# First slice of embedding rows normed and projected on its own, ahead of the lag network's last layer, in a one-core language-model tower

## What is computed

```python
h = W[x] + pe                                   # embedding
n = (h - mean(h)) / sqrt(var(h) + 1e-5)         # first layer norm
q, k, v = n @ Wq.T, *split(n @ Wkv.T)
q, k = elu(q) + 1, elu(k) + 1                   # = max(x, 0) + exp(min(x, 0))
D = 1 / max(einsum(q, k.sum(tokens)), 1e-6)
context = einsum('bhnd,bhne->bhde', k, v)
h = h + (einsum('bhnd,bhde->bhne', q, context) * D) @ Wproj.T + bproj
...
g = idx @ pos_w.T + pos_b                       # the lag network, used by the third block
for i in range(3):
    g = relu(g / (norm(g) / sqrt(8) + 1e-8)) @ rpe_lw[i].T + rpe_lb[i]
a = relu(g / (norm(g) / sqrt(8) + 1e-8)) @ out_w.T + out_b
```

## Time and profile before

| | |
|---|---|
| median of 3 runs | 337.44 us (334.92 to 338.07) |
| the profiled execution: its time | 338.1 us |
| its span from first to last instruction | 336.4 us |
| TensorE busy | 302.3 us, 90% of the span |
| VectorE busy | 231.2 us, 69% |
| ScalarE busy | 147.5 us, 44% |
| GpSimd busy | 118.7 us, 35% |
| chain that ended last | TensorE 52%, VectorE 10%, GpSimd 5%, ScalarE 3% |

### The profile page before, as it was taken

The page is one execution under the profiler, slowest core; times in us unless marked ns, Lnnn a source line. Parts: engine busy times, 40 slices in busy tenths (PEclk is TensorE's granted clock), DMA queues, the critical chain, the costliest instruction groups (busy, mean ns, idle before and its releaser), DMA issues.

```text
span 336.4 us, 4468 instructions
## 1 busy us (share of the span) xinstructions
PE 302.3 (90%) x1598; PEld 171.7 (51%) x1598; DVE 231.2 (69%) x420; ACT 147.5 (44%) x246; POOL 118.7 (35%) x167
## 2 busy tenths in 40 slices
PE   1649879999989999989899999999999999999884
PEld 1316654653333434667545556554555555557552
DVE  1578788799988684276854687744678577673676
ACT  2113543933766676455546444544532110022452
POOL 5764001332741245201402550431004689900114
PEclk9999999999999999998999999999999999999959
DMA  7959300483000003300000000000000000000001
GB/s 249 320 99 365 141 0 0 69 155 61 3 2 3 2 2 113 140 2 0 1 0 2 0 1 2 0 0 2 1 0 2 0 0 2 0 0 1 2 0 63
DMA packets 6270, 15.17 MB, mean 45 GB/s; under 512 B 1384, under 2 KB 3816, under 8 KB 5608
## 3 DMA queue, kind: packets, MB, share of 16 engines
q1 hardware_dynamic: 5685, 14.35, 14.3%
q0 software_dynamic: 512, 0.53, 0.7%
q10 hardware_dynamic: 51, 0.01, 0.0%
HBM read 11.95 MB, written 0.52 MB: 37 GB/s over the span
## 4 chain that ended last, share of the span: by engine, by line
PE 52%; DVE 10%; POOL 5%; ACT 3%; issue 2%; POOLq 0%; DVEq 0%; ACTq 0%
PE ps L325 50%; DVE arena L1856 1%; DVE h L1982 1%; POOL share L587 1%; ACT L1197 1%; PE ps L1098 1%; DVE xs L1784 1%; DVE rw L1727 1%; POOL share L588 1%; ACT arena L1304 1%; POOL st L551 0%; POOL rw L480 0%; DVE arena L1777 0%; DVE xc L2044 0%; PE ps L872 0%
## 5 line engine op out<-in xcount | busy, mean ns | idle before, releaser
L1727 DVE TENSOR_REDUCE rw<-ps 128x1 f32<-128x512 f32 (+2 forms) x80 | 45.8, 629 | 6.9 <-PE ps L325 6.4
L1315 ACT ACTIVATE arena<-ps 128x1024 f32<-128x1024 f32 (+3 forms) x48 | 37.6, 812 | 24.6 <-PE ps L325 24.1
L325 PE MATMUL ps<-arena 96*128 96x512 bf16 (+7 forms) x192 | 42.8, 327 | 0.6 <-DVE rw L1727 0.2
L1375 ACT ACTIVATE arena<-ps 128x512 f32<-128x512 f32 x48 | 28.7, 598 | 29.1 <-PE ps L325 24.8
L325 PE MATMUL ps<-xs,e_hi 128*128 128x512 f32 x96 | 41.1, 428 | 0.2 <-DVE arena L1856 0.2
L1856 DVE TENSOR_TENSOR arena<-ps,arena 128x512 f32<-128x512 f32 x48 | 32.6, 687 | 11.5 <-ACT arena L1375 10.0
L325 PE MATMUL ps<-xs,e_lo 128*128 128x512 f32 x96 | 38.4, 400 | 0.0
L325 PE MATMUL ps<-bfc_s 128*128 128x512 bf16 (+2 forms) x112 | 30.8, 356 | 1.7 <-issue 1.7
L325 PEld LDWEIGHTS ps<-arena 96*128 96x128 bf16 (+1 forms) x192 | 15.9, 98 | 26.5 <-DVE rw L1727 11.6
L494 POOL TENSOR_SCALAR_AFFINE_SELECT arena<-arena 128x256 f32<-128x256 f32 (+1 forms) x32 | 15.0, 472 | 33.3 <-ACT arena L1315 32.8
L325 PE MATMUL ps<-w,xT 128*128 128x128 f32 (+2 forms) x160 | 23.3, 329 | 2.7 <-ACT xT L1359 1.1
(11 more groups left out here) (266 smaller groups left out, 515.6 us busy)
## 6 DMA issues: line engine op xcount, KB each, us to landing
arena<-arena SPq DMA_DIRECT2D x24, 96.0 KB, 2.8
arena<-tm SPq DMA_DIRECT2D x2, 1024.0 KB, 5.9
w<-wpack SPq DMA_DIRECT2D x1, 2025.5 KB
tables<-epack SPq DMA_DIRECT2D x1, 1540.0 KB, 11.0
arena<-rope SPq DMA_DIRECT2D x1, 1024.0 KB
tables<-tu SPq DMA_DIRECT2D x2, 512.0 KB, 4.0
tables<-tk SPq DMA_DIRECT2D x2, 512.0 KB, 6.1
rp<-rpack SPq DMA_DIRECT2D x1, 678.5 KB, 4.2
```

Source lines behind the costliest of these rows:

```text
L325: return nc.tensor.matmul(o, l, r, start=start, stop=stop, **kw)
L1315: nc.scalar.activation(pt[:, n % PT_SLOTS, :, lo:512], ps[:, bank:bank + 2, lo:512], ACT.Exp, scale=HD ** -0.5).then_inc(S("exp_done"), 1)
L1375: nc.scalar.activation(sil[:, m % 2], ps[:, m % 2], ACT.Silu).then_inc(S("silu"), 1)
L1727: V.tensor_reduce(top_view(m, part)[:, at:at + len(heads), i], src, AXX, ALU.max, negate=True).then_inc(S("ring_read"), 1)
```

## The change

- The lag network's last layer is cut in pieces. DVE runs layers 0 to 2, then `embed(0)`, and only then the last layer's square. The rest of that layer (scale, reciprocal, product) stands behind `embed(1)`.
- The first half of the rows gets its own sum of squares (`first_total(0)`), its own root on ACT (`first_root`, which takes 1/C and epsilon itself, from a new tile `eps1`), its own reciprocal and scaling (`first_scale(0)`). TensorE transposes and projects it at once (`first_projections(0)`: 4 transposes, 4 matmuls each for keys and values, one for the queries), ahead of the lag rows' transposes. The second half follows after `embed(2)`.
- ACT copies both halves of the transposed rows, and for the first half takes the keys' and queries' minima as relu(-x); exp then has scale -1.
- `keep_warm` has 10 matmuls in place of 14 and waits for the third centred slice.
- POOL's addition of `bproj` also waits for the last `geo` table. Semaphore values behind it move by one.

```diff
             pool.wait_ge(S("n1"), 2)
+            pool.wait_ge(S("geo_done"), 2 * NW)
...
+            def first_projections(a):
+                pe.wait_ge(S("n1"), a + 1)
+                for j in range(4 * a, 4 * a + 4):
+                    ins = nc.tensor.transpose(ps[:, 2 + a, j % 4 * P:(j % 4 + 1) * P], sq[:, j].rearrange("p b c -> p (b c)"), idt[:])
+                ins.then_inc(S("T1"), 1)
+                pe.wait_ge(ld_w, 16)
+                pe.wait_ge(S(("xT1_lo", "xT1_hi")[a]), 1)
+                for x in range(2):
+                    for j in range(4 * a, 4 * a + 4):
+                        ins = mm(ps[:, 2 * x + a, j % 4 * P:(j % 4 + 1) * P], xT[:, j * P:(j + 1) * P], W("kv1", x * P, (x + 1) * P))
+                    ins.then_inc(S("kv1"), 1)
+                mm(ps[:, 4 + a], W("q1"), xT[:, a * 512:(a + 1) * 512]).then_inc(S("q1"), 1)
+
+            first_projections(0)
             pe.wait_ge(S("r_act"), LAYERS + 1)
             nc.tensor.transpose(ps[:, 7, 0:P], rh[:, 3, 0:P], idt[:])
             nc.tensor.transpose(ps[:, 7, P:2 * P], rh[:, 3, P:2 * P], idt[:]).then_inc(S("r_T"), 1)
             pe.wait_ge(ld_bf, 16)
-            pe.wait_ge(S("first_centred"), 1)
-            keep_warm(14, 6)
-            transposes(sq, 2, S("n1"), S("T1"))
...
+            pe.wait_ge(S("first_centred"), 3)
+            keep_warm(10, 6)
+            first_projections(1)
...
+            for i in range(LAYERS):
+                lag_root(i)
+            first_squares(0)
+            lag_root(LAYERS)
+            act.wait_ge(S("geo_constants"), 1)
+            first_root(0)
+            first_columns(0)
+            first_squares(1)
+            act.wait_ge(S("kv1"), 1)
+            nc.scalar.activation(kf1[:, 0:4].rearrange("p j b c -> p (j b c)"), ps[:, 0], ACT.Relu, scale=-1.0).then_inc(S("kmin"), 1)
+            first_values(0)
+            act.wait_ge(S("q1"), 1)
+            nc.scalar.activation(qf1[:, 0:512], ps[:, 4], ACT.Relu, scale=-1.0).then_inc(S("qmin"), 1)
+            first_squares(2)
+            first_root(1)
             next_function(ACT.Exp)
+            first_columns(1)
...
-            for i in range(LAYERS + 1):
+            for i in range(LAYERS):
                 rpe_layer(i)
             dve.wait_ge(ld_pe, 16)
             embed(0)
+            V.tensor_tensor(rh[:, 1], rh[:, 0], rh[:, 0], ALU.mult).then_inc(S("r_sq"), 1)
+            first_total(0)
+            first_scale(0)
             embed(1)
-            first_sums(0)
+            dve.wait_ge(S("r_rms"), LAYERS + 1)
+            V.scalar_tensor_tensor(out=scale_r, in0=scale_r, scalar=1e-8, in1=rh[:, 2], op0=ALU.mult, op1=ALU.add).then_inc(S("r_scale"), 1)
+            dve.wait_ge(S("r_scale"), LAYERS + 1)
+            step(V.reciprocal(scale_r, scale_r))
+            V.scalar_tensor_tensor(out=rh[:, 3], in0=rh[:, 0], scalar=0.0, in1=scale_r, op0=ALU.max, op1=ALU.mult).then_inc(S("r_act"), 1)
+            first_sums(1)
             embed(2)
-            first_sums(1)
-            first_sums(2)
-            V.tensor_scalar(st[:, 2], st[:, 1], 1.0 / C, 1e-5, ALU.mult, ALU.add).then_inc(S("mean_squares"), 1)
-            dve.wait_ge(S("roots"), NORMS["std1"])
-            step(V.reciprocal(st[:, 4], st[:, 3]))
-            scale_rows(sq, xc, 4, S("n1"))
-            evac(3, S("T1"), 2, S("xT1_hi"))
             dve.wait_ge(S("r_T"), 1)
             step(V.tensor_copy(rh[:, 1], ps[:, 7, 0:2 * P]))
+            first_total(2)
+            first_scale(1)
```

More of the change, by code:

```diff
@@ L289, in build @@
         unused = sb("unused", [1, 16])
+        eps1 = sb("eps1", [P, 1])
         halves = sb("halves", [P, 8])
@@ L1215, in _ @@
                 nc.scalar.activation(rh[:, 2], ps[:, 0, 0:2 * P], ACT.Sqrt, scale=1.0 / R).then_inc(S("r_rms"), 1)
[L1216 to L1221, removed]
-            next_function(ACT.Exp)
-            for a in range(2):
-                act.wait_ge(S("kmin"), a + 1)
-                nc.scalar.activation(kf1[:, 4 * a:4 * a + 4], kf1[:, 4 * a:4 * a + 4], ACT.Exp).then_inc(S("kexp"), 1)
@@ L1226, in _, with first_root @@
-            for a in range(2):
-                act.wait_ge(S("kv1"), a + 3)
-                nc.scalar.copy(va1[:, 4 * a:4 * a + 4, 0:P], ps[:, 2 + a].rearrange("p (j x) -> p j x", j=4)).then_inc(S("va1"), 1)
-            for c in range(2):
-                act.wait_ge(S("qmin"), c + 1)
-                nc.scalar.activation(qf1[:, c * 512:(c + 1) * 512], tmp[:, c * 512:(c + 1) * 512], ACT.Exp).then_inc(S("qexp"), 1)
+            def first_root(a):
+                act.wait_ge(S("mean_squares"), NORMS["var1"] + a)
+                nc.scalar.activation(st[:, 3, 8 * a:8 * a + 8], st[:, 1, 8 * a:8 * a + 8], ACT.Sqrt, scale=1.0 / C,
+                                     bias=eps1[:]).then_inc(S("roots"), 1)
@@ new lines, in _ @@
+            first_squares(2)
+            first_root(1)
+            next_function(ACT.Exp)
+            first_columns(1)
+            act.wait_ge(S("kmin"), 1)
+            nc.scalar.activation(kf1[:, 0:4], kf1[:, 0:4], ACT.Exp, scale=-1.0).then_inc(S("kexp"), 1)
+            act.wait_ge(S("qmin"), 1)
+            nc.scalar.activation(qf1[:, 0:512], qf1[:, 0:512], ACT.Exp, scale=-1.0).then_inc(S("qexp"), 1)
+            act.wait_ge(S("kmin"), 2)
+            nc.scalar.activation(kf1[:, 4:8], kf1[:, 4:8], ACT.Exp).then_inc(S("kexp"), 1)
@@ L1232, in _ @@
+            first_values(1)
+            act.wait_ge(S("qmin"), 2)
+            nc.scalar.activation(qf1[:, 512:N], tmp[:, 512:N], ACT.Exp).then_inc(S("qexp"), 1)
             next_function(ACT.Sqrt)
@@ L1545, in _ @@
             dve.wait_ge(ld_rp, 16)
+            V.memset(eps1[:], 1e-5)
             V.memset(geo[:], 0.0).then_inc(S("geo_constants"), 1)
@@ L1591, in first_sums, with first_scale, first_total @@
                 step(V.tensor_reduce(st[:, 1, B * lo:B * hi], sq[:, lo:hi].rearrange("p j b c -> p (j b) c"), AXX, ALU.add))
-            for i in range(LAYERS + 1):
+            def first_scale(a):
+                dve.wait_ge(S("roots"), NORMS["std1"] + a)
+                step(V.reciprocal(hst(4, a), hst(3, a)))
+                V.tensor_tensor(half3(sq, a), half3(xc, a), spread(hst(4, a), 2, C), ALU.mult).then_inc(S("n1"), 1)
+            def first_total(a):
+                lo, hi = SLICES[a]
+                dve.wait_ge(S("first_squared"), a + 1)
+                V.tensor_reduce(st[:, 1, B * lo:B * hi], sq[:, lo:hi].rearrange("p j b c -> p (j b) c"), AXX,
+                                ALU.add).then_inc(S("mean_squares"), 1)
+            for i in range(LAYERS):
                 rpe_layer(i)
@@ L1629, in _ @@
                                        op1=ALU.add).then_inc(S("kf1"), 1)
[L1630 to L1632 removed]
+            dve.wait_ge(S("kv1"), 3)
+            V.tensor_scalar(k2[:, 512:N], ps[:, 1], 0.0, None, ALU.min).then_inc(S("kmin"), 1)
+            key_features(0)
+            dve.wait_ge(S("q1"), 2)
+            V.tensor_scalar(tmp[:, 512:N], ps[:, 5], 0.0, None, ALU.min).then_inc(S("qmin"), 1)
+            key_features(1)
             def query_features(c):
```

45 lines of the change are left out of this document (16 added, 29 removed).

## The result

| | before | after |
|---|---|---|
| median | 336.36 us (4 runs, 334.92 to 338.07) | 341.96 us (4 runs, 339.14 to 343.72) |
| profiled execution: time, span | 338.1, 336.4 us | 342.35, 340.6 us |
| the mark, start of the queries times the context | 38.29 us | 42.58 us |
| last instruction of VectorE | 333.22 us | 337.46 us |

The changed kernel is slower: ratio 1.016, 95% interval 1.0097 to 1.0222. Of the profiled pair, the mark is 4.29 us later and VectorE's last instruction 4.24 us. So the whole loss of the trace is there at the mark, and nothing behind it hides or adds to it. The medians differ by 5.6 us; their interval (3.3 to 7.5 us) contains both. The two profiled executions had the same mean granted clock, 0.98, so their stretches behind the mark can be compared.

What follows compares the result with a forecast made beforehand. VectorE was taken to set the pace up to the mark, with late gathers behind SyncE's loads. Second half 5.5 us late minus 1.6 from the split gave +3.9, 341.3 us on the medians' scale; range 338.0 to 342.8.

Steps and rivals of the forecast that it cites:

- The cover goes: VectorE before `embed(0)`: with the last lag layer moved behind, it idles 4.1 us for late gathers, starting at 20.1.
- The first half: From `embed(0)` through squares, sum, root and scaling: `first_root(0)` queues behind ACT's lag root; first half ready at 25.4 us.
- The new wait: VectorE waits from 30.9 to 32.6 us for lag transposes, behind first-half projections at TensorE's lower clock, 5.1 us.
- The second half: After the lag transposes: copy, last sum, root, reciprocal and scaling make it ready at 34.9 us, 5.5 late.
- What the split gives back: From scaled rows to the mark only one half is left: 7.3 us in place of 8.9, 1.6 less.
- The relu: First half's minima on ACT: takes two passes of about 0.6 us off VectorE, inside its wait, so brings nothing.
- POOL's wait: POOL's 2.35 us addition starts at about 36, ends at 38.3, before its reader at 43; costs nothing.
- Nothing hides the loss further on: Behind the mark: no wait seen that hides the +3.9 us; the rival that one does, 337.4 us, had chance 0.06.
- The first rival: Gathers complete by 16 us but TensorE late: mark 0 to +1 us, 337.4 to 338.4 us; chance 0.10.

Runs made afterwards that it cites:

- loads_late: Changed kernel with SyncE's loads of weights and masks held until the first slice is gathered, rotary tables until all gathers are done; mark 38.72 us (42.58 in the changed kernel).
- lag_first_clock: lag_first plus nine `keep_warm` matmuls between the lag transposes and the first half's; mark 40.60 us (42.73 in lag_first).
- clock_up3: Changed kernel with six unread 256-column fp32 matmuls before the last lag sum and four `keep_warm` matmuls ahead of `first_projections(0)`; mark 41.65 us (42.58 in the changed kernel).
- minima_dve: Changed kernel with the first half's key and query minima back on VectorE, in place of ScalarE's two relu; mark 42.72 us (42.58 in the changed kernel).
- pool_behind: Kernel before the change, with only GpSimd's addition of bproj made to wait for the lag table; mark 38.46 us (38.29 before).
- lag_first: Changed kernel with the last lag layer whole again before `embed(0)`, its transposes before the first half's projections; mark 42.73 us (42.58 in the changed kernel).
- clock_up2: Changed kernel with nine unread 256-column fp32 matmuls on TensorE in front of the last lag sum; mark 44.08 us (42.58 in the changed kernel).

## Why the prediction was right

Forecast 341.3 us, +3.9 at the mark; measured 341.96 us and +4.29. The mechanism came as forecast. That the median came so close is in part luck: the forecast stands on a median before of 337.44 us (3 runs), which is 336.36 with the fourth run. The medians differ by 5.6 us, not by 3.9.

- *The cover goes.* Forecast: `embed(0)` at 20.1, idle for 4.1 us. Measured: 19.67, idle for 3.81. loads_late confirms both the cause and the reading of the packet counts, and holding back the loads gives back 3.9 us of the loss.
- *The first half.* Forecast ready at 25.4 with ScalarE's `first_root` behind the lag root; measured 24.99, with both rows side by side at 23.46 and 23.74.
- *The new wait.* Forecast: projections at the lower clock 5.1 us, done at 32.3, VectorE waits 1.7. Measured: 26.93 to 32.18, 5.25 us, then a wait of 2.31. This term was mis-sized by some tenths: the clock rose only after the projections' end, so that they ran low for all their length. The wait is 0.6 us longer than forecast because, besides, VectorE came to it at 30.52, not at 30.9. lag_first_clock shows the clock's effect by one edit, and clock_up3 shows that it passes to the mark.
- *The second half.* Forecast 34.9, measured 35.14. *What the split gives back*: forecast 7.3 us from there to the mark, measured 7.44, against 8.93 before. So 5.5 - 1.6 was forecast, and 5.8 - 1.5 came.
- *The relu* was priced at nothing: the waits in minima_dve agree. *POOL's wait* was priced at nothing as well; it does free VectorE of half a microsecond beside the lag table, which I had not priced, and which pool_behind shows to be worth nothing there.
- *Nothing hides the loss further on*: 4.29 at the mark, 4.24 at the end.
- *The first rival* (gathers in time, TensorE late) was priced at a mark of 38.2 to 39.2. loads_late made that kernel: 38.72.

What the sum did not say is how its terms stand to each other. I wrote 5.5 us as a chain in which the displaced lag layer stands, which suggests that putting the layer back would return it. lag_first shows that it returns nothing: displaced layer and slow projections lie side by side. The first ends with `embed(2)` at 30.5 us, the second with the lag transposes at 32.8, and the queries' relu ties ScalarE to the second. The forecast number came from the later of the two, so it held; a repair read off the sum would have failed. What both begin with is the late first slice, and loads_late, which takes away that alone, nearly restores the mark.

## What to carry to other kernels

Before work is moved forward to "while the gathers run", count when the gather's packets begin, not when it is issued: behind bulk loads the first slice's last packets began after 18 us here, and before 15 us without the loads, and the work moved aside had been the cover. When two chains lie side by side, undoing the one that ends first gives nothing (lag_first), while taking away what both begin with gives nearly all (loads_late). A fixed order couples the halves it splits: each instruction of the second half that is queued behind one of the first (squares behind relu, lag transposes behind projections) inherits the first half's slow clock.

## What was not expected of the hardware

- Unread matmuls can raise the clock too early and cost time: nine fp32 ones of 256 columns came with a lag root at 25.5 us in place of 23.5 (clock_up2), though the modelled rows end at 19.7; with six it started at 23.47 (clock_up3). Why is not known.
- The clock can fall when TensorE is at work again, and not in the gap. The fillers of clock_up3 end by the rows at 18.7, and TensorE idles to 22.7. The lag sum then still ran at the upper level (0.70 us), the granted clock went to 0.50 between 23 and 24 us, and it stayed there to about 30, over four `keep_warm` matmuls and most of the projections. Nine `keep_warm` matmuls directly ahead of the transposes (lag_first_clock), themselves at the lower level, had it up for the projections at 27.53.
- A GpSimd addition of 2.35 us stretched a VectorE subtraction with two SBUF inputs from 0.29 to 0.78 us (pool_behind against before).
